# Mamba output projection: the residual goes through TensorE as an identity product, ScalarE copies the sum out, and TensorE waits for the gate's own signal

## Chip, cores and metric

One NeuronCore of a Trainium2 chip runs the whole program. The time is the device time of one execution in microseconds; the median of three runs of the kernel before is 5767.12 us (5765.01 to 5771.17). All data are float32.

## What is computed

The reference is four stacked blocks on x (4 sequences, 512 positions, width 256) with a context of 64 positions. The first block is a Mamba stack of four layers, and the change lies in it; the other three are transformer layers and stay as they are. The Mamba part, cut to what matters:

```python
p = silu(prepend_cond @ pre_w1) @ pre_w2
h = concatenate([p, x], axis=1)                 # 64 + 512 = 576 positions
for l in range(4):
    h = h + mamba_block(rmsnorm(h, norm_w[l]), ...)

def mamba_block(x, ...):
    xi, z = split(x @ ip_w.T)                   # 512 channels each
    xi = silu(causal_conv(xi) + cb)
    dt, Bm, Cm = split(xi @ xp_w.T)
    dt = softplus(dt @ dtp_w.T + dtp_b)
    # 16 states for every channel:
    #   state = exp(dt * A) * state + dt * Bm * xi ;  y += Cm * state
    y = y + xi * Dp
    y = y * silu(z)                             # the gate
    return y @ op_w.T                           # the output projection, then "h +" above
```

## The kernel before

Channels (or the model's 256 features, in KD = 2 halves) lie on the 128 partitions and the T = 576 positions along the free dimension. `hT` (named "stream" in the profile) holds h, the residual stream, in SBUF for all four sequences. The work is cut into 16 units (4 layers x 4 sequences), and the unit n is scanned in window n. A window has NJ = 32 steps, numbered j: 2 halves h of 256 channels (HC = 1152 elements per partition) times 16 states. In every step

- VectorE makes the drive (`drive`, L620, writes U in PSUM) and then runs the recurrence (`recur`, L628, writes the step's UH buffer in SBUF),
- ScalarE has made the decay factors DA for it (`decay`, L507; the decay for step j + 2 is issued in step j and may run four scans ahead),
- GpSimd multiplies UH by Cm (L561) while VectorE is in a later step,
- TensorE adds the result to Y in PSUM by a product with the identity IDENT (`add_up`, L357). `add_up(j - 2)` is issued in step j.

There are five UH buffers (four from step 20 on), so scan j waits until the sum of the step that last used its buffer is done; there are four DA buffers. Into the same window n every engine's queue has the preparation of unit n + 1 (`prep_step`, `prep_read`: norm, input projection, convolution, softplus) and the end of unit n - 1 woven in by hand: `PREP_AT` and `END_AT` say at which j. Each queue is a fixed program order and all ordering between engines goes by counting semaphores.

The end of a unit is the gate and the output projection. The gate (`gate`, L635) multiplies half the Y sums by silu(z) into ZS; half 0 is gated at j = 17 of the unit's own window, half 1 at j = 2 of the next one. The first `add_up` of the following half overwrites Y, so it waits for the gate. The output projection (`project`, two uses "O", m = 0 at j = 6 and m = 1 at j = 8 of the next window) writes PAIR, one pair of PSUM banks that all preparation products share too: every use waits on `s_free`, which the reader of the use before raises. Its product rows all show L313, the line of the helper `halves`. On VectorE `add(m)` (L642) adds PAIR to the residual at j = 7 and j = 9 and raises `s_free`, and after m = 1 `s_tail`, which the next read of that part of the stream waits for. Window 0 scans and has no end part; windows 1 to 15 have both; window 16 is only the end of unit 15. After it come the final RMS norm and the transformer layers.

Of the kernel before, what the change touches and what calls it, by code (L numbers as in the profile page):

```python
# [10 lines left out]
P = 128  # L11
# [90 lines left out]
def mamba_stack(nc, hT, IDENT, wa, wb, x_t, ctx_t, pre_w, ones, fin_norm):  # L102
# [3 lines left out]
    with ctx:  # L106
# [8 lines left out]
        def step(name):  # L115
            steps.append(sem(name))
            return steps[-1]
# [59 lines left out]
        s_scan = step("s_scan")  # L177
        s_hc = step("s_hc")
        s_y = step("s_y")
        s_gate = step("s_gate")  # L180
        s_add = step("s_add")
        s_yv = step("s_yv")
        s_tail = step("s_tail")
# [6 lines left out]
        def half(ap):  # L190
            return ap.rearrange("p (a n) -> p a n", a=2)
# [16 lines left out]
        with nc.Block() as block:  # L208
# [65 lines left out]
            def _(pe):  # L274
# [23 lines left out]
                def body(n, scan, prep, end):  # L298
                    uses, base = window_uses(prep, end), before(n, N_PREP, N_END)
                    par = n % 2  # L300
                    nxt = n + 1
                    npar = nxt % 2
                    done = [0]

                    def use(kind, i):
                        assert uses[done[0]] == (kind, i)
                        if scan or end or done[0]:
                            pe.wait_ge(s_free, START + base + done[0])
                        done[0] += 1

                    def halves(out_rows, lhs, rhs, start, stop):
                        for a in range(2):
                            mm = pe.matmul(PAIR[0:out_rows, a, 0:HT], lhs, rhs(a), start=start, stop=stop)  # L313
                        return mm

                    def cut(ap):
                        return lambda a: ap[:, a * HT:(a + 1) * HT]

                    def prep_step(kind, i):
                        use(kind, i)  # L320
                        if kind == "ms":
                            pe.wait_ge(s_sq, START + nxt + 1)
                            for k in range(KD):
                                mm = halves(P, ONES[:, :], cut(HN[:, k, :]), k == 0, k == KD - 1)
                        if kind == "xz":
                            if i == 0:
                                pe.wait_ge(s_wa, 16 * nxt + 16)
                                pe.wait_ge(s_hn, START + nxt + 1)
                            for k in range(KD):
                                mm = halves(P, w_in[:, k, i * P:(i + 1) * P], cut(HN[:, k, :]), k == 0, k == KD - 1)  # L330
                        if kind == "cv":
                            pe.wait_ge(s_xi, START + nxt * KI + i + 1)
                            if i == 0:
                                pe.wait_ge(s_pad, START + nxt + 1)
                                pe.wait_ge(s_dg, START + nxt // NB + 1)
                            for j in range(DC):
                                mm = halves(P, DG[:, i, j, :],
                                            lambda a, j=j: XPAD[:, i, j + a * HT:j + (a + 1) * HT], j == 0, j == DC - 1)
                        if kind == "xp":
                            pe.wait_ge(s_xs, START + nxt + 1)  # L340
                            for k in range(KI):
                                mm = halves(NXP, w_xp[:, k, :],
                                            lambda a, k=k: XS[:, bass.ds(npar * (KI * T) + k * T + a * HT, HT)],
                                            k == 0, k == KI - 1)
                        if kind == "dt":
                            if i == 0:
                                pe.wait_ge(s_bcf, START + nxt + 1)
                            mm = halves(P, w_dto[:, i * P:(i + 1) * P], cut(BCF[NBC:NXP, :]), True, True)
                        mm.then_inc(s_full, 1)

                    def add_up(j, of):
                        h, s = j // DS, j % DS
                        if s == 0:
                            pe.wait_ge(s_gate, START + 2 * of + h)
                        pe.wait_ge(s_hc, START + of * NJ + j + 1)
                        for a, b in YSEG:
                            mm = pe.matmul(Y[:, a:b], IDENT[:, :], UH[:, SLOT[j], a:b],  # L357
                                           start=(s == 0), stop=(s == DS - 1), skip_group_check=True)
                        mm.then_inc(s_y, 1)
                        if s == 0:  # L360
                            x = of % 2 * (KI * T) + h * HC
                            for c, a, b in DSEG:
                                pe.matmul(Y[:, a:b], DD[:, of // NB % 2, h * HK + c, :], XS[:, x + a:x + b],
                                          start=False, stop=False, skip_group_check=True)

                    def project(m):
                        use("O", m)
                        if m == 0:
                            pe.wait_ge(s_yv, START + 2 * n)
                            pe.wait_ge(s_wb, 16 * n)  # L370
                        epar = (n - 1) % 2
                        for k in range(KI):
                            mm = halves(P, w_out[:, k, m * P:(m + 1) * P],
                                        lambda a, k=k: ZS[:, bass.ds(epar * (KI * T) + k * T + a * HT, HT)],
                                        k == 0, k == KI - 1)
                        mm.then_inc(s_full, 1)

                    for j in range(NJ):
                        if end and j < 2:
                            add_up(NJ - 2 + j, n - 1)  # L380
                        for kind, i in slot_uses(j, prep, end):
                            if kind == "O":
                                project(i)
                            else:
                                prep_step(kind, i)
                        if scan and j >= 2:
                            add_up(j - 2, n)
# [11 lines left out]
            def _(act):  # L399
# [12 lines left out]
                def body(n, scan, prep, end):  # L412
# [26 lines left out]
                    def prep_read(kind, i):  # L439
# [24 lines left out]
                        if kind == "dt":  # L464
# [9 lines left out]
                            if i == KI - 1:  # L474
                                own(act.activation(ALOG[:, :], WA[:, A_LOG:A_COLS], ACT.Exp))
                                act.activation(NEGA[:, bass.ds(npar * (KI * DS), KI * DS)], ALOG[:, :], ACT.Copy,
                                               scale=-1.0).then_inc(s_nega, 1)

                    def diagonals(h):
                        if h == 0:  # L480
                            act.wait_ge(s_wa, 16 * nxt + 16)
                        for c in range(h * HK, h * HK + HK):
                            for j in range(DC):
                                w = A_CONV + c * DC + j
                                act.activation(DG[:, c, j, :], IDENT[:, :], ACT.Copy, scale=WA[:, w:w + 1])
                            ins = act.activation(DD[:, nxt // NB % 2, c, :], IDENT[:, :], ACT.Copy,
                                                 scale=DV[:, nxt // NB, c:c + 1])
                        if h:
                            ins.then_inc(s_dg, 1)
# [27 lines left out]
                    for j in range(NJ):  # L517
# [8 lines left out]
                        if prep and j in (2, 3) and nxt % NB == 0:  # L526
                            diagonals(j - 2)
                        for kind, i in slot_uses(j, prep, end):
                            if kind != "O":
                                prep_read(kind, i)  # L530
                    assert not prep or step[0] == k0, step
                act.wait_ge(s_zero, START + 3)
# [33 lines left out]
            def _(dve):  # L566
                def body(n, scan, prep, end):
# [63 lines left out]
                    def gate(of, h, at):  # L631
                        dve.wait_ge(s_y, START + of * NJ + DS * (h + 1))
                        dve.wait_ge(s_zs, START + of + 1)
                        z = ZS[:, bass.ds(at + h * HC, HC)]
                        dve.tensor_tensor(z, Y[:, 0:HC], z, ALU.mult).then_inc(s_yv, 1)  # L635
                        dve.wait_ge(s_yv, START + 2 * of + h + 1)
                        dve.sem_inc(s_gate, 1)

                    def add(m):
                        dve.wait_ge(s_full, START + base + uses.index(("O", m)) + 1)  # L640
                        h = hT[:, m, bass.ds(((n - 1) % NB) * T, T)]
                        dve.tensor_tensor(half(h), half(h), pair, ALU.add).then_inc(s_add, 1)  # L642
                        dve.wait_ge(s_add, START + (n - 1) * KD + m + 1)
                        dve.sem_inc(s_free, 1)  # L644
                        if m == KD - 1:
                            dve.sem_inc(s_tail, 1)

                    if scan:
                        dve.wait_ge(s_dt, START + n + 1)
                    for j in range(NJ):  # L650
# [7 lines left out]
                        if prep and j == 3:  # L658
                            norm()
                            pad()  # L660
                        if end and j in (7, 9):
                            add((j - 7) // 2)
                        if prep and j in SOFTPLUS:
                            softplus(*SOFTPLUS[j])
                    assert step[0] == (k_prep if prep else 0), step
# [990 lines left out]
```

## Time and profile before

| | us |
|---|---|
| median of 3 runs | 5767.12 |
| profiled execution | 5772.53 |
| its span on the core | 5770.7 |
| VectorE busy over the span | 3934.4 (68%) |
| TensorE busy over the span | 5049.1 (87%) |
| ScalarE busy over the span | 2275.0 (39%) |
| GpSimd busy over the span | 2549.6 (44%) |

The shares mix two stages: the Mamba stage ends at about 2520 us, the transformer layers fill the rest. The chain of work that ended last, as the profile gives it, adds up to 56% of the span and so covers only the transformer part; for the Mamba stage the timeline and the groups of instructions have to be read instead. In the forty slices of the page VectorE's digit is 9 from the second slice to the seventeenth.

### The profile page before, as it was taken

Reading aid. Unit: us, or ns where it says so; the run is one execution under the profiler, and the core shown is the slowest. Engines: PE = TensorE matmul, PEld = TensorE weight load, DVE = VectorE, ACT = ScalarE, POOL = GpSimd, SP = SyncE. Lnnn points to the kernel's source line nnn. Section 1 sums busy time; section 2 is a strip of 40 time slices with the busy share of each in tenths; the row PEclk is TensorE's granted clock in tenths of the full one; section 3 lists DMA queues with packets and bytes.
Section 4 is the critical chain, followed back from the end, with each engine's and each line's share of the span. In section 5 each row is a group of like instructions: output and inputs, shape, how many; then the busy total and the mean of one; then the engine's idle time right before and its main releaser. Section 6 shows DMA issues by size and latency. Waiting matters only on the chain.

```text
span 5770.7 us, 53704 instructions
## 1 busy us (share of the span) xinstructions
PE 5049.1 (87%) x18992; PEld 2658.1 (46%) x18992; DVE 3934.4 (68%) x3924; ACT 2275.0 (39%) x3972; POOL 2549.6 (44%) x1292
## 2 busy tenths in 40 slices
PE   6888888888888888669998799999978999999889
PEld 3445555455555555334444444444444444444444
DVE  2999999999999999946665515555454155554541
ACT  4555545555555554324343223333322133333221
POOL 1555555555555555527773004666400056664000
PEclk8999999999999999879999899999999999999999
DMA  2334433444344344310001000000101000001000
GB/s 82 139 141 142 145 135 136 144 144 143 141 142 146 141 145 140 133 46 1 1 1 37 26 11 1 1 1 1 44 1 37 0 1 1 1 1 44 1 0 15
DMA packets 94440, 376.70 MB, mean 65 GB/s; under 512 B 13025, under 2 KB 14433, under 8 KB 91233
## 3 DMA queue, kind: packets, MB, share of 16 engines
q1 hardware_dynamic: 94176, 373.26, 18.3%
q8 instruction: 157, 2.57, 0.2%
q14 instruction: 107, 0.87, 0.0%
HBM read 369.94 MB, written 3.28 MB: 65 GB/s over the span
## 4 chain that ended last, share of the span: by engine, by line
PE 45%; DVE 6%; POOL 2%; ACT 2%; issue 1%; DMA 0%; SPq 0%; ACTq 0%; DVEq 0%
PE PS L1010 6%; PE PS L1020 6%; PE PS L1034 6%; PE PS L989 5%; PE PS L1176 5%; PE PS L1185 3%; PE PS L1142 3%; PE PS L998 3%; PE PS L1044 2%; POOL PA L957 2%; PE PS L1116 2%; PE PS L1125 1%; DVE CST L1476 1%; DVE PA L1478 1%; PE PS L968 1%; DVE PA L1489 1%
## 5 line engine op out<-in xcount | busy, mean ns | idle before, releaser
L561 POOL TENSOR_TENSOR UH<-UH,BC 128x1152 f32<-128x1152 f32 x512 | 1343.0, 2623 | 1124.4 <-DVE U L620 1124.4
L957 POOL TENSOR_SCALAR PA<-PA,INV 128x512 f32<-128x512 f32 x768 | 1188.5, 1563 | 1296.5 <-DVE INV L1408 1296.5
L357 PE MATMUL Y<-UH,ident_sb 128*128 128x512 f32 (+1 forms) x3072 | 1180.1, 528 | 262.9 <-POOL UH L561 211.4
L628 DVE TENSOR_TENSOR_SCAN UH<-DA,U 128x1152 f32<-128x1152 f32 x512 | 1307.2, 2553 | 21.2 <-ACT DA L507 3.8
L357 PEld LDWEIGHTS Y<-UH,ident_sb 128*128 128x128 f32 x3072 | 593.0, 203 | 891.2 <-issue 571.2
L507 ACT ACTIVATE DA<-DT,NEGA 128x575 f32<-128x575 f32 x1024 | 722.9, 764 | 484.8 <-DVEq L612 259.9
L1247 ACT ACTIVATE PA<-PS,NMX 128x512 f32<-128x512 f32 x768 | 520.4, 682 | 981.4 <-DVE NMX L1402 968.5
L620 DVE TENSOR_TENSOR U<-DTX,BC 128x1152 f32<-128x1152 f32 x512 | 701.5, 1370 | 60.3 <-DVE stream L642 8.0
L1402 DVE TENSOR_REDUCE NMX<-PS 128x2 f32<-128x1024 f32 x384 | 468.0, 1219 | 296.4 <-PE PS L1010 296.4
L1417 DVE COPY VP<-PS 128x512 f32<-128x512 f32 x768 | 491.8, 681 | 15.0 <-PE PS L1020 14.6
L1020 PEld LDWEIGHTS PS<-ident_sb,PA 128*128 128x128 f32 x3072 | 329.4, 142 | 317.0 <-issue 214.7
L1020 PE MATMUL PS<-ident_sb,PA 128*128 128x128 f32 x3072 | 438.3, 282 | 9.4 <-POOL PA L957 8.6
L1010 PE MATMUL PS<-QK 64*128 64x512 f32 (+1 forms) x1536 | 435.4, 644 | 4.8 <-issue 2.5
L1034 PE MATMUL PS<-VP 128*64 128x256 f32 (+1 forms) x3072 | 373.9, 385 | 4.2 <-DVE VP L1417 2.5
L989 PE MATMUL PS<-HN,W 128*128 128x512 f32 x640 | 309.8, 606 | 54.9 <-ACTq L1240 52.0
L1394 DVE TENSOR_SCALAR QK<-PS,VEC 128x512 f32<-128x512 f32 x80 | 64.8, 810 | 347.1 <-PE PS L989 347.1
L313 PE MATMUL PAIR<-HN,WA 128*128 128x288 f32 x1024 | 280.4, 418 | 21.8 <-DVE HN L588 6.4
L1176 PE MATMUL PS<-HN,VP 128*128 128x512 f32 x640 | 288.6, 592 | 4.5 <-issue 4.5
L313 PE MATMUL PAIR<-XPAD,DG 128*128 128x288 f32 x1024 | 259.8, 406 | 3.3 <-ACTq L457 1.8
L1034 PEld LDWEIGHTS PS<-VP 128*64 128x64 f32 (+1 forms) x3072 | 202.2, 128 | 123.8 <-issue 38.1
L313 PEld LDWEIGHTS PAIR<-HN,WA 128*128 128x128 f32 x1024 | 189.6, 195 | 73.7 <-DVEq L644 8.0
L1519 DVE SCALAR_TENSOR_TENSOR QK<-PS,VEC,QK 128x512 f32<-128x512 f32 x64 | 48.1, 751 | 250.2 <-ACT QK L1326 250.2
(124 smaller groups left out, 5249.3 us busy)
## 6 DMA issues: line engine op xcount, KB each, us to landing
BC<-bc_rows SPq DMA_DIRECT2D x512, 576.0 KB, 3.7
WA<-mamba_a SPq DMA_DIRECT2D x16, 1421.0 KB, 7.4
W<-pair_w SPq DMA_DIRECT2D x6, 3072.0 KB, 10.6
WB<-mamba_b SPq DMA_DIRECT2D x16, 514.0 KB, 5.0
VP<-ff_w SPq DMA_DIRECT2D x2, 3072.0 KB
WO<-out_w SPq DMA_DIRECT2D x4, 1024.0 KB
stream<-x_t SPq DMA_DIRECT2D x2, 1024.0 KB, 6.7
VP<-ff_w SPq DMA_DIRECT2D x2, 1024.0 KB
```

Source lines behind the costliest of these rows:

```text
L313: mm = pe.matmul(PAIR[0:out_rows, a, 0:HT], lhs, rhs(a), start=start, stop=stop)
L357: mm = pe.matmul(Y[:, a:b], IDENT[:, :], UH[:, SLOT[j], a:b], start=(s == 0), stop=(s == DS - 1), skip_group_check=True)
L507: ins = act.activation(DA[:, j % NDA, c * T + 1:(c + 1) * T], DT[:, bass.ds(par * (KI * T) + cc * T + 1, T - 1)], ACT.Exp, scale=NEGA[:, b ...
L561: pool.tensor_tensor(h, h, BC[:, j % NBB, 1, :].unsqueeze(1).broadcast_to([P, HK, T]), ALU.mult).then_inc(s_hc, 1)
L620: dve.tensor_tensor(u, x, BC[:, j % NBB, 0, :].unsqueeze(1).broadcast_to([P, HK, T]), ALU.mult).then_inc(s_u, 1)
L628: dve.tensor_tensor_scan(UH[:, SLOT[j], :], DA[:, j % NDA, :], U[:, 0:HC], 0.0, ALU.mult, ALU.add).then_inc(s_scan, 1)
L957: pool.tensor_scalar(PR[:, n % 3, j, :], PR[:, n % 3, j, :], INV[:, n % 4, j:j + 1], None, ALU.mult).then_inc(s_ps, 1)
L989: mm = pe.matmul(PS[:, B_J, :], w_tile(l, "qk".index(kind), t, k), HN[:, k, b * S0:(b + 1) * S0], start=(k == 0), stop=(k == KD - 1))
L1010: mm = pe.matmul(PS[:, B_S + 2 * (n % 2) + j, :], Q[r:r + HW[l], tt % 2, qt * P:(qt + 1) * P], K[r:r + HW[l], tt % 2, :], start=True, stop ...
L1020: mm = pe.transpose(PS[:, B_T + j, kt * P:(kt + 1) * P], PR[:, n % 3, j, kt * P:(kt + 1) * P], IDENT[:, :])
L1034: mm = pe.matmul(PS[r:r + HW[l], B_V, half * 256:(half + 1) * 256], VT[:, tt // QT % 2, kt, c:c + HW[l]], PT[:, hh % 2, kt, j, :], start=( ...
L1176: mm = pe.matmul(PS[:, 2 * (f % 2) + g, :], w1[:, k, c:c + P], HN[:, k, b * S0:(b + 1) * S0], start=(k == 0), stop=(k == KD - 1))
```

## The change

The last product of each projection use no longer closes the sum. A product of IDENT with the residual itself follows into the same PAIR banks and closes it, so PAIR then holds h + y @ op_w. ScalarE copies PAIR over the residual (`stream(m)`), in its own queue at steps 6 and 8, and raises `s_free` and `s_tail`. VectorE's `add` is gone. VectorE's gate no longer waits for its own completion to raise a second semaphore `s_gate`; TensorE's first sum of a half waits on `s_yv`, which the gate instruction raises itself.

```diff
-                            pe.wait_ge(s_gate, START + 2 * of + h)
+                            pe.wait_ge(s_yv, START + 2 * of + h)
...
                         for k in range(KI):
                             mm = halves(P, w_out[:, k, m * P:(m + 1) * P],
                                         lambda a, k=k: ZS[...],
-                                        k == 0, k == KI - 1)
+                                        k == 0, False)
+                        mm = halves(P, IDENT[:, :], cut(hT[:, m, bass.ds(((n - 1) % NB) * T, T)]), False, True)
                         mm.then_inc(s_full, 1)
...
+                    def stream(m):
+                        full("O", m)
+                        act.activation(half(hT[:, m, bass.ds(((n - 1) % NB) * T, T)]), pair, ACT.Copy).then_inc(s_add, 1)
+                        act.wait_ge(s_add, START + (n - 1) * KD + m + 1)
+                        act.sem_inc(s_free, 1)
+                        if m == KD - 1:
+                            act.sem_inc(s_tail, 1)
...
-                            if kind != "O":
+                            if kind == "O":
+                                stream(i)
+                            else:
                                 prep_read(kind, i)
...
                         dve.tensor_tensor(z, Y[:, 0:HC], z, ALU.mult).then_inc(s_yv, 1)
-                        dve.wait_ge(s_yv, START + 2 * of + h + 1)
-                        dve.sem_inc(s_gate, 1)
-
-                    def add(m):
-                        dve.wait_ge(s_full, START + base + uses.index(("O", m)) + 1)
-                        h = hT[:, m, bass.ds(((n - 1) % NB) * T, T)]
-                        dve.tensor_tensor(half(h), half(h), pair, ALU.add).then_inc(s_add, 1)
-                        dve.wait_ge(s_add, START + (n - 1) * KD + m + 1)
-                        dve.sem_inc(s_free, 1)
-                        if m == KD - 1:
-                            dve.sem_inc(s_tail, 1)
...
-                        if end and j in (7, 9):
-                            add((j - 7) // 2)
```

VectorE's queue in window 1 of the kernel before, from the drive of step 2 over the gate and the two adds (L635 is the gate, L642 the adds, L620 drives, L628 scans):

```order
96 L620 TENSOR_TENSOR U<-DTX,BC 128x1152 [waits s_scan,s_bc2]
97 L628 SCALAR_TENSOR_TENSOR UH<-DA,U 128x1152 [waits s_y,s_da,s_u]
98 L635 TENSOR_TENSOR ZS<-Y,ZS 128x1152 [waits s_zs,s_y]
99 L620 TENSOR_TENSOR U<-DTX,BC 128x1152 [waits s_yv,s_scan,s_bc3]
...
111 L628 SCALAR_TENSOR_TENSOR UH<-DA,U 128x1152 [waits s_y,s_da,s_u]
112 L642 TENSOR_TENSOR stream<-stream,PAIR 128x576 [waits s_full]
113 L620 TENSOR_TENSOR U<-DTX,BC 128x1152 [waits s_add,s_scan,s_bc0]
...
116 L628 SCALAR_TENSOR_TENSOR UH<-DA,U 128x1152 [waits s_y,s_da,s_u]
117 L642 TENSOR_TENSOR stream<-stream,PAIR 128x576 [waits s_full]
118 L620 TENSOR_TENSOR U<-DTX,BC 128x1152 [waits s_add,s_scan,s_bc2]
```

The same stretch of VectorE's queue in the changed kernel, whose lines are ten higher here:

```order
96 L630 TENSOR_TENSOR U<-DTX,BC 128x1152 [waits s_scan,s_bc2]
97 L638 SCALAR_TENSOR_TENSOR UH<-DA,U 128x1152 [waits s_y,s_da,s_u]
98 L645 TENSOR_TENSOR ZS<-Y,ZS 128x1152 [waits s_zs,s_y]
99 L630 TENSOR_TENSOR U<-DTX,BC 128x1152 [waits s_scan,s_bc3]
...
111 L638 SCALAR_TENSOR_TENSOR UH<-DA,U 128x1152 [waits s_y,s_da,s_u]
112 L630 TENSOR_TENSOR U<-DTX,BC 128x1152 [waits s_scan,s_bc0]
113 L638 SCALAR_TENSOR_TENSOR UH<-DA,U 128x1152 [waits s_y,s_da,s_u]
114 L630 TENSOR_TENSOR U<-DTX,BC 128x1152 [waits s_scan,s_bc1]
```

The adds and their waits are gone, and the drive behind the gate no longer waits on s_yv. TensorE's queue in the same window, kernel before, from the last preparation product ahead of the projection to the first one behind it:

```order
200 L313 MATMUL PAIR<-HN,WA 128x288 [waits s_free]
201 L313 MATMUL PAIR<-HN,WA 128x288 x3
...
205 L313 MATMUL PAIR<-ZS,WB 128x288 [waits s_wb,s_yv,s_free]
206 L313 MATMUL PAIR<-ZS,WB 128x288 x7
207 L357 MATMUL Y<-UH,ident_sb 128x512 [waits s_hc]
...
213 L313 MATMUL PAIR<-ZS,WB 128x288 [waits s_free]
214 L313 MATMUL PAIR<-ZS,WB 128x288 x7
...
221 L313 MATMUL PAIR<-HN,WA 128x288 [waits s_free]
```

And in the changed kernel:

```order
200 L312 MATMUL PAIR<-HN,WA 128x288 [waits s_free]
201 L312 MATMUL PAIR<-HN,WA 128x288 x3
...
205 L312 MATMUL PAIR<-ZS,WB 128x288 [waits s_wb,s_yv,s_free]
206 L312 MATMUL PAIR<-ZS,WB 128x288 x7
207 L312 MATMUL PAIR<-stream,ident_sb 128x288 x2
208 L356 MATMUL Y<-UH,ident_sb 128x512 [waits s_hc]
...
214 L312 MATMUL PAIR<-ZS,WB 128x288 [waits s_free]
215 L312 MATMUL PAIR<-ZS,WB 128x288 x7
216 L312 MATMUL PAIR<-stream,ident_sb 128x288 x2
...
223 L312 MATMUL PAIR<-HN,WA 128x288 [waits s_free]
```

Each projection has grown by two products; nothing else moved on TensorE.

## Rows read from the trace of the kernel before

**Rows 1.** Windows view: length, busy time of each engine, PEclk, DMA share, GB/s.

```profile
100.00:2400.00 2300.00, 1945.17 (x6222) 1143.05 (x6221) 2216.26 (x1253) 1190.65 (x1607) 1293.42 (x493) 0.92 0.40 140
```

**Rows 2.** Groups on VectorE from 100 to 2400 us: busy us, mean ns, idle before.

```profile
L620 DVE TENSOR_TENSOR U<-DTX,BC 128x1152 f32<-128x1152 f32 x495 | 678.3, 1370 | 58.4 <-DVE stream L642 8.0 <-DVE ZS L635 6.4 <-DVEq L612 3.9
...
L635 DVE TENSOR_TENSOR ZS<-Y,ZS 128x1152 f32<-128x1152 f32 x30 | 39.9, 1331 | 0.0
...
L642 DVE TENSOR_TENSOR stream<-stream,PAIR 128x576 f32<-128x576 f32 x30 | 21.8, 728 | 0.0
```

**Rows 3.** Timeline of VectorE around both adds, window 6: start, length, instruction.

```profile
1034.87 1.37 DVE L620 TENSOR_TENSOR U<-DTX,BC 128x1152 f32<-128x1152 f32 x1
...
1038.74 0.73 DVE L642 TENSOR_TENSOR stream<-stream,PAIR 128x576 f32<-128x576 f32 x1
1039.68 1.37 DVE L620 TENSOR_TENSOR U<-DTX,BC 128x1152 f32<-128x1152 f32 x1 [0.21 <-DVE stream L642]
...
1043.74 1.37 DVE L620 TENSOR_TENSOR U<-DTX,BC 128x1152 f32<-128x1152 f32 x1
...
1047.61 0.73 DVE L642 TENSOR_TENSOR stream<-stream,PAIR 128x576 f32<-128x576 f32 x1
1048.66 1.37 DVE L620 TENSOR_TENSOR U<-DTX,BC 128x1152 f32<-128x1152 f32 x1 [0.32 <-DVE stream L642]
```

**Rows 4.** Timeline of VectorE: norm, gate and softplus, each with the drive behind it.

```profile
1021.16 1.61 DVE L588 SCALAR_TENSOR_TENSOR HN<-stream,WA,RSTD 128x576 f32<-128x576 f32 x2
1022.71 1.34 DVE L620 TENSOR_TENSOR U<-DTX,BC 128x1152 f32<-128x1152 f32 x1
...
1080.94 1.33 DVE L635 TENSOR_TENSOR ZS<-Y,ZS 128x1152 f32<-128x1152 f32 x1
1082.49 1.37 DVE L620 TENSOR_TENSOR U<-DTX,BC 128x1152 f32<-128x1152 f32 x1 [0.21 <-DVE ZS L635]
...
1142.44 1.36 DVE L605 SCALAR_TENSOR_TENSOR XPAD<-XPAD 128x1152 f32<-128x1152 f32 x1
1143.84 1.37 DVE L620 TENSOR_TENSOR U<-DTX,BC 128x1152 f32<-128x1152 f32 x1
```

**Rows 5.** Timeline of TensorE around both projections, window 6.

```profile
1030.99 4.05 PE L313 MATMUL PAIR<-ZS,WB 128*128 128x288 f32 x16
1034.87 4.04 PE L357 MATMUL Y<-UH,ident_sb 128*128 128x512 f32 x12
1039.58 4.15 PE L313 MATMUL PAIR<-ZS,WB 128*128 128x288 f32 x16 [0.67 <-DVEq L644]
1043.56 4.04 PE L357 MATMUL Y<-UH,ident_sb 128*128 128x512 f32 x12
1048.45 1.72 PE L313 MATMUL PAIR<-HN,WA 128*128 128x288 f32 x6 [0.85 <-DVEq L644]
```

**Rows 6.** Timeline of ScalarE, window 6: decay of step 11, and a copy of PAIR.

```profile
1038.85 1.44 ACT L507 ACTIVATE DA<-DT,NEGA 128x575 f32<-128x575 f32 x2 [2.62 <-DVE UH L628]
...
1050.70 0.65 ACT L446 ACTIVATE XPAD<-PAIR 128x576 f32<-128x576 f32 x1 [5.59 <-PE PAIR L313]
```

**Rows 7.** Timeline of VectorE, window 6: the scans of steps 23 and 24.

```profile
1104.18 2.55 DVE L628 TENSOR_TENSOR_SCAN UH<-DA,U 128x1152 f32<-128x1152 f32 x1
...
1108.24 2.55 DVE L628 TENSOR_TENSOR_SCAN UH<-DA,U 128x1152 f32<-128x1152 f32 x1
```

**Rows 8.** Timeline of ScalarE: the decays of steps 23 and 24.

```profile
1098.73 2.77 ACT L507 ACTIVATE DA<-DT,NEGA 128x575 f32<-128x575 f32 x4
```

**Rows 9.** Timeline of TensorE: the sum of step 20.

```profile
1101.54 2.21 PE L357 MATMUL Y<-UH,ident_sb 128*128 128x512 f32 x6
```

**Rows 10.** Timeline of the last window, all engines: first projection, its add, the second projection.

```profile
2480.16 4.12 PE L313 MATMUL PAIR<-ZS,WB 128*128 128x288 f32 x16 [1.50 <-issue]
2484.31 0.75 DVE L642 TENSOR_TENSOR stream<-stream,PAIR 128x576 f32<-128x576 f32 x1 [4.26 <-PE PAIR L313]
2485.18 4.15 PE L313 MATMUL PAIR<-ZS,WB 128*128 128x288 f32 x16 [0.90 <-DVEq L644]
```

More of the change, by code:

```diff
@@ L179, in mamba_stack @@
         s_y = step("s_y")
-        s_gate = step("s_gate")
         s_add = step("s_add")
```

## The prediction, made before the run

> **What bounds the kernel now.** I began with the busy time of each engine over the Mamba stage. From 100 to 2400 us VectorE is busy 2216.3 of 2300 us, that is 96%, while TensorE has 1945.2, GpSimd 1293.4 and ScalarE 1190.7 [rows 1]. The whole program's 68% for VectorE hides this, because the transformer layers dilute it. Next I asked what VectorE's idle time there is made of. The groups show it in crumbs: the drive, L620, has 58.4 us before 495 instructions, of which 8.0 lie behind the adds, 6.4 behind the gates and 3.9 behind softplus; the rest is the regular gap between scan and drive [rows 2]. No other engine is named as a large releaser. So in this stage the VectorE queue itself is the clock. The timeline shows its beat: the drive of step 8 starts at 1039.68 and that of step 9 at 1043.74, 4.06 us later, and no other engine is in between [rows 3]. What leaves this queue comes off the time, as long as nobody else becomes late. The transformer layers start after the stage and keep their length.
>
> **The adds leave VectorE.** A step without an add takes 4.06 us from drive to drive. The step with the first add takes 1039.68 - 1034.87 = 4.81, the one with the second 1048.66 - 1043.74 = 4.92 [rows 3]. That is 0.75 and 0.86, or 1.61 us a window, although the instruction itself lasts 0.73: it starts before the scan's end is reported, but the drive behind it waits for the add's completion and for one or two separate semaphore increments (0.21 and 0.32 idle). Fifteen windows have both a scan and an end part, so 15 x 1.61 = **24.2 us** come off.
>
> **The gates lose their own wait.** The gate lasts 1.33, but the drive behind it starts 1.55 us after the gate starts, 0.21 or 0.22 after its end [rows 4]. Without the wait on itself and the increment, two neighbours bound what is left. Behind softplus the drive also waits for its predecessor's completion, but with no separate increment, and starts 1143.84 - 1142.44 = 1.40 after it, 0.04 after its end; that would save 0.18. Behind the norm there is no wait for completion at all, and the drive starts 1.55 after the norm's start, with 1.61 of work reported, so 0.06 before its end [rows 4]; that would save 0.28. The changed gate is of the second kind, since the drive's remaining waits (scan, BC rows) are met long before. I take 0.27. There are 16 gates of half 0 and 15 of half 1 with a drive behind them: 31 x 0.27 = **8.4 us**, between 5.6 and 8.7.
>
> Here a rule of the Trainium skill speaks against the gate's part. The rows above show 0.21 behind the gate against 0.04 behind softplus. The page "VectorE: DVE Perf Modes", section "The DRAIN you can't avoid", says that an instruction waits for the pipeline to empty anyway, and that "the semaphore costs nothing extra here". By that the gate's part would be worth nothing, and the sum would be 22.4 instead of 30.8. The trace bears it out for the plain wait (0.04) and not for the wait with an increment of its own (0.21), so I keep 8.4.
>
> **TensorE's new work.** A projection is 16 recorded products, and the next group starts 1034.87 - 1030.99 = 3.88 later, 0.243 each [rows 5]. The identity product of the residual adds two float32 products of 288 columns, four records: 0.97 us each time, 1.94 a window. What hides it is that TensorE waited in just these places for VectorE's add to free PAIR: 0.67 before the second projection and 0.85 before the preparation product behind it, 1.52 together [rows 5]. Placed in order: projection 0 from 1030.99 to 1035.84, the two sums to 1039.71, projection 1 (before: 1039.58) to 1044.56, the two sums to 1048.43, next product (before: 1048.45). TensorE comes out of the stretch where it did. VectorE, however, is then 1.61 + 0.27 = 1.9 us ahead, so TensorE's lead over the scans shrinks by up to that.
>
> How much lead is there? The nearest case in the window is scan 24, which needs the UH buffer whose last sum, step 20, ends at 1101.54 + 2.21 = 1103.75; the scan starts at 1108.24 [rows 7, 9]. The lead is 4.5 us. If the whole 1.9 and the second gate's 0.27 came off it, 2.3 would be left. I cost the added products at nothing; without that cover each microsecond would cost 15 over the stage. PAIR also comes free earlier than before, since ScalarE copies it at once and not behind a scan.
>
> **ScalarE's new work.** Two copies of PAIR to SBUF of 128x576, like the one at L446 that takes 0.65 [rows 6]: 1.3 us a window on an engine busy 1190.7 of 2300 [rows 1]. What matters is what stands behind a copy that waits. In the queue, `stream(0)` stands ahead of the decay for step 9 and `stream(1)` ahead of the decay for step 11. The latter ran at 1038.85 [rows 6]; now it waits for projection 1 (1044.6 plus its tail), the copy ends near 1045.6 and the decay near 1047.1. Scan 11 starts, on the beat of rows 3, at 1048.66 + 4.06 + 1.40 = 1054.1 before, so near 1052.2 now: 5.1 us of lead instead of 13.8. The tightest decay is that of step 23: two decays share the 2.77 from 1098.73, so the first ends near 1100.1, and scan 23 starts at 1104.18 [rows 7, 8]. Its lead of 4.0 shrinks by the same 2.2 at most, to 1.8. It is behind TensorE's convolutions and ScalarE's SiLU, and it still holds. Cost: nothing.
>
> **TensorE's first sums of a half** hear the gate one increment earlier, some 0.1 us. TensorE isn't the bound, so nothing.
>
> **The last window** has no scan to hide anything. Projection, reader, projection, reader stand in line [rows 10]. Each projection grows by 0.97, each copy replaces an add of 0.75 by 0.65: 2 x (0.97 - 0.1) = **1.8 us** slower.
>
> **Sum.** -24.2 - 8.4 + 1.8 = -30.8. The profiled execution took 5772.53 with a span of 5770.7, so 1.8 lies outside the span. Its successor should have a span near 5739.9 and take 5741.7. The median of the runs shown, 5767.12, lies 5.4 below the profiled one, which I take over: 5767.1 - 30.8 = **5736.3 us**. Runs of before differ by 6 us among each other; a difference under 0.2%, 11.5 us, could hardly be told from none.
>
> **Rivals.**
>
> 1. *The wait behind the gate stays.* The gap after the gate is then the pipeline's own. Against it stands 0.04 behind softplus [rows 4]. Time: 5767.1 - 22.4 = 5744.7. Chance 0.10.
>
> 2. *ScalarE's copies slow VectorE.* They read PSUM and write SBUF while scans and drives run, where VectorE itself did it before. The rows show drives at a mean of 1.370 with ScalarE busy half of the time [rows 1, 2], so contention is small. If each of 30 copies cost a VectorE instruction 0.23, 7 us would go back: 5743. Chance 0.05.
>
> 3. *The lead is used up, the time hardly moves.* The scans come to wait for sums or for decays around steps 20 to 24. To fall inside 0.2%, (30.8 - 11.5) / 15 = 1.3 us must be lost in each window; with 1.8 left there, the lead must have shrunk by 3 us more than I work out, for instance because the SiLU and the decays queue up behind later TensorE work. Time from 5755.6 to 5767. Chance 0.05.
>
> 4. *Slower: the decays behind a waiting copy.* Place: ScalarE's queue in step 8, where the decay for step 11 now stands behind projection 1. It decides once that projection ends more than 5.1 us later than 1044.6. That would come about if TensorE ran this stretch at the lower of its clock levels, 1.2 GHz: 2 x 4.85 for each projection and 2 x 3.87 for the sums between puts its end at 1058.1, the decay's at 1060.5 against a scan at 1052.2, so 8.3 are lost and 2.1 won in each of 15 windows: +93, plus 1.8 in the tail, less what the gate of half 0 gives: near 5860. Against it stands that products there run at 0.243 each [rows 5], and that TensorE now waits less in this stretch, not more. Mean granted clock is 0.92 [rows 1]. Chance 0.03.
>
> **How the numbers follow.** The forecast has 0.77. It and the first two rivals are all faster by more than 0.2%: 0.92. Rival 3 gives the same: 0.05, rival 4 slower: 0.03. The gate's bounds alone move the sum from 28.0 to 31.1. Around the forecast I add the runs' own spread of some 4 us to both sides, and a little more below for beats that the rows round: 5727. Above, the range reaches over rivals 1 and 2 with part of that spread: 5748.
>
> **What would show it.** In the profile after, VectorE's adds are absent and drive to drive is 4.06 in steps 7 and 9 (adds right). The drive starts within 0.05 us of the gate's end or before it (gate right); 0.2 behind it speaks for rival 1. The projection is a group of 20 records, 4.85 to the next group, and no TensorE idle time has VectorE's increment as its releaser (cover right). Scans show no idle time released by ScalarE or TensorE (lead right; otherwise rivals 3 or 4). A window, from the drive of step 0 to the next such drive, shrinks by 2.1 us. I would be wrong if that period shrank less while VectorE's busy time fell as expected; then a wait at L638 would name the engine. Or the transformer part, untouched, could shift by a few us with TensorE's clock.

## The result and the profile after

The changed kernel takes 5743.82 us (median of 5 runs, 5739.52 to 5745.58), against 5767.17 us (5 runs, 5765.01 to 5771.17). The ratio is 0.9958 with a 95% interval of 0.9943 to 0.9972, which is 16 to 33 us; the medians give 23 us, the ratio 24. The forecast was 30.8 us faster, 5736.3, with a range of 5727 to 5748. The profiled execution took 5742.71 with a span of 5740.9, 29.8 below the profiled one of before. Not all of that belongs to the change. From the first drive of window 0 to the memset of the tile KB, with which the transformer layers begin, the kernel before needs 2522.67 - 112.25 = 2410.4 us and the changed one 2496.11 - 109.43 = 2386.7, so 23.7 less. The other 6 lie ahead of the stage (first drive at 109.4 instead of 112.3) and in the transformer layers (3244.8 instead of 3248.1), which no edit touches. In the twelve profiles of this study these layers take 3241.9 to 3249.2 us.

The groups on VectorE from 100 to 2400 us in the changed kernel, columns as in [rows 2]:

```profile
L630 DVE TENSOR_TENSOR U<-DTX,BC 128x1152 f32<-128x1152 f32 x502 | 687.4, 1369 | 48.4 <-DVEq L622 4.2 <-DVE UH L638 1.9
...
L645 DVE TENSOR_TENSOR ZS<-Y,ZS 128x1152 f32<-128x1152 f32 x31 | 41.5, 1338 | 4.6 <-PE Y L356 4.6
```

The adds are gone, and so is the idle time behind adds and gates. But ahead of the gate, L645, where VectorE had no idle time before [rows 2], it now has 4.6 us that ended with a sum of TensorE (L356). That is a new wait. The timeline of VectorE in window 6, gate of half 1 and then the drives of steps 7 and 8, answers to [rows 3, 4]:

```profile
1003.50 1.33 DVE L645 TENSOR_TENSOR ZS<-Y,ZS 128x1152 f32<-128x1152 f32 x1
1004.75 1.35 DVE L630 TENSOR_TENSOR U<-DTX,BC 128x1152 f32<-128x1152 f32 x1
...
1022.30 1.37 DVE L630 TENSOR_TENSOR U<-DTX,BC 128x1152 f32<-128x1152 f32 x1
...
1026.36 1.37 DVE L630 TENSOR_TENSOR U<-DTX,BC 128x1152 f32<-128x1152 f32 x1
```

The step with the first add takes 4.06 now (it took 4.81), and the drive starts 1.25 after the gate's start instead of 1.55, 0.08 before the gate's end. TensorE in the same window, answering to [rows 5]:

```profile
1020.37 4.05 PE L312 MATMUL PAIR<-ZS,WB 128*128 128x288 f32 x16
1024.26 1.13 PE L312 MATMUL PAIR<-stream,ident_sb 128*128 128x288 f32 x4
1025.23 4.04 PE L356 MATMUL Y<-UH,ident_sb 128*128 128x512 f32 x12
1029.10 4.05 PE L312 MATMUL PAIR<-ZS,WB 128*128 128x288 f32 x16
1032.99 1.13 PE L312 MATMUL PAIR<-stream,ident_sb 128*128 128x288 f32 x4
1033.96 4.04 PE L356 MATMUL Y<-UH,ident_sb 128*128 128x512 f32 x12
1037.83 2.11 PE L312 MATMUL PAIR<-HN,WA 128*128 128x288 f32 x8
```

From the first projection to the preparation product behind the second pass 1037.83 - 1020.37 = 17.46 us, exactly as in window 6 of the kernel before (1048.45 - 1030.99). The added 0.97 a time is visible (1025.23 - 1024.26), and the two waits for VectorE are gone; no row has idle time. Window 6 of the kernel before is not like all others, though. In its window 5 the same stretch reads:

```profile
884.39 4.05 PE L313 MATMUL PAIR<-ZS,WB 128*128 128x288 f32 x16
...
892.15 4.05 PE L313 MATMUL PAIR<-ZS,WB 128*128 128x288 f32 x16
...
900.24 1.97 PE L313 MATMUL PAIR<-HN,WA 128*128 128x288 f32 x7 [0.17 <-DVEq L644]
```

TensorE is 1.6 us later behind the gate there (first projection 16.8 after it, 15.2 in window 6), so it hardly waits for the adds, and the stretch takes 15.85. Of the fourteen windows 1 to 14 of the kernel before only 2, 4, 6, 8 and 10 have the waits of 1.52; the other nine have 0 to 0.32 and stretches of 15.5 to 16.0. In the changed kernel the stretch takes 17.46 in all fourteen, 1.5 to 1.9 more than in those nine.

ScalarE in window 6 of the changed kernel:

```profile
1025.43 0.65 ACT L481 ACTIVATE stream<-PAIR 128x576 f32<-128x576 f32 x1 [4.58 <-PE PAIR L312]
1026.20 2.77 ACT L515 ACTIVATE DA<-DT,NEGA 128x575 f32<-128x575 f32 x4
1034.16 0.65 ACT L481 ACTIVATE stream<-PAIR 128x576 f32<-128x576 f32 x1 [5.19 <-PE PAIR L312]
1035.00 2.77 ACT L515 ACTIVATE DA<-DT,NEGA 128x575 f32<-128x575 f32 x4 [0.19 <-ACT stream L481]
```

ScalarE does wait 4.6 and 5.2 us for the projections, and decays stand behind it in pairs, but no scan of windows 1 to 15 shows idle time put down to them. Now step 17 of this window, the place of the new wait, all engines:

```profile
1062.88 1.37 DVE L630 TENSOR_TENSOR U<-DTX,BC 128x1152 f32<-128x1152 f32 x1
...
1063.07 4.04 PE L356 MATMUL Y<-UH,ident_sb 128*128 128x512 f32 x12
...
1064.29 2.55 DVE L638 TENSOR_TENSOR_SCAN UH<-DA,U 128x1152 f32<-128x1152 f32 x1
...
1067.15 1.36 DVE L645 TENSOR_TENSOR ZS<-Y,ZS 128x1152 f32<-128x1152 f32 x1 [0.31 <-PE Y L356]
1068.42 1.36 DVE L630 TENSOR_TENSOR U<-DTX,BC 128x1152 f32<-128x1152 f32 x1
```

The sums of steps 14 and 15 run as one group without a gap and end at 1067.11; the gate starts 0.04 later. It should have started 0.08 before the scan's end (1066.84), at 1066.76, so VectorE loses 0.39. In the kernel before the sum of step 15 of this window reads:

```profile
1077.19 2.21 PE L357 MATMUL Y<-UH,ident_sb 128*128 128x512 f32 x6 [1.30 <-POOL UH L561]
```

It ended at 1079.40, 1.54 us ahead of the gate (1080.94 [rows 4]), after TensorE had waited 1.30 for GpSimd. The lead is 1.5 in all fourteen windows there.

How much is lost differs between windows, and the difference begins far earlier. TensorE where its sums resume after the gate of half 1, first in window 6, then in window 8:

```profile
1004.89 2.96 PE L356 MATMUL Y<-UH,ident_sb 128*128 128x512 f32 x6 [3.45 <-DVE ZS L645]
1007.64 3.20 PE L362 MATMUL Y<-XS,DD 128*128 128x512 f32 x8
```

```profile
1297.50 2.21 PE L356 MATMUL Y<-UH,ident_sb 128*128 128x512 f32 x6 [2.99 <-DVE ZS L645]
1299.54 2.22 PE L362 MATMUL Y<-XS,DD 128*128 128x512 f32 x8
```

The windows view of these stretches (columns as in [rows 1]):

```profile
1004.80:1010.60 5.80, 5.71 (x14) 2.99 (x15) 5.76 (x7) 1.60 (x3) 2.61 (x1) 0.71 0.39 127
1297.40:1301.50 4.10, 4.00 (x14) 2.19 (x15) 4.07 (x4) 1.61 (x3) 2.62 (x1) 1.00 0.42 143
1010.00:1068.00 58.00, 58.00 (x211) 37.24 (x210) 55.86 (x31) 25.65 (x37) 36.81 (x14) 1.00 0.42 152
```

In window 6 TensorE resumes at a mean granted clock of 0.71, so partly at 1.2 GHz, after waits of 5.80 us ahead of the norm's product and 3.45 for the gate; in window 8 it resumes at 1.00, 2.4 GHz, after waits of 3.80 and 2.99. That costs 5.8 against 4.1 us, and from there to 1068 it is busy 58.00 of 58.00 us: nothing absorbs the late start. The fourteen windows sort without exception. Where the first input product comes 7.4 us after the gate of half 1 starts (7, 8, 10, 11, 13, 14), the sum is done 1.35 ahead of the gate of half 0 and VectorE loses nothing. Where it comes 9.1 after (1 to 6) it loses 0.37 to 0.40, and where it comes 10.3 or 10.4 after (9 and 12) 1.58 and 1.32. Together 5.2 us. The mean granted clock from the first sum behind the gate to that input product is 1.00 in the first group, 0.78 in the second and 0.66 to 0.67 in the third.

The last window, answering to [rows 10]:

```profile
2450.33 4.12 PE L312 MATMUL PAIR<-ZS,WB 128*128 128x288 f32 x16 [1.50 <-issue]
2454.28 1.13 PE L312 MATMUL PAIR<-stream,ident_sb 128*128 128x288 f32 x4
2455.45 0.65 ACT L481 ACTIVATE stream<-PAIR 128x576 f32<-128x576 f32 x1 [27.44 <-PE PAIR L312]
2456.20 4.15 PE L312 MATMUL PAIR<-ZS,WB 128*128 128x288 f32 x16 [0.79 <-ACTq L483]
```

One projection follows the other after 5.87 us, it was 5.02 [rows 10].

### The profile page after: what moved, and what is told of

It reads as the page before. It is cut to its first block, busy times and chain, and to the rows that moved or that the text cites. A ratio compares the mean times of both kernels' runs of the same rounds, so it can differ in the third digit from the quotient of the medians.

```text
span 5740.9 us, 53927 instructions
## 1 busy us (share of the span) xinstructions
PE 5059.7 (88%) x19120; PEld 2676.5 (47%) x19120; DVE 3911.5 (68%) x3892; ACT 2293.0 (40%) x4004; POOL 2553.2 (44%) x1292
## 4 chain that ended last, share of the span: by engine, by line
PE 45%; DVE 6%; POOL 2%; ACT 2%; issue 1%; DMA 0%; SPq 0%; ACTq 0%; DVEq 0%
PE PS L1007 6%; PE PS L1017 6%; PE PS L1031 6%; PE PS L986 5%; PE PS L1173 5%; PE PS L1182 3%; PE PS L1139 3%; PE PS L995 3%; PE PS L1041 2%; POOL PA L954 2%; PE PS L1113 2%; PE PS L1122 1%; DVE CST L1473 1%; DVE PA L1475 1%; PE PS L965 1%; DVE PA L1486 1%
## 5 line engine op out<-in xcount | busy, mean ns | idle before, releaser
L356 PE MATMUL Y<-UH,ident_sb 128*128 128x512 f32 (+1 forms) x3072 | 1174.3, 527 | 226.9 <-POOL UH L571 172.2
L356 PEld LDWEIGHTS Y<-UH,ident_sb 128*128 128x128 f32 x3072 | 592.4, 203 | 847.5 <-issue 571.9
L630 DVE TENSOR_TENSOR U<-DTX,BC 128x1152 f32<-128x1152 f32 x512 | 701.1, 1369 | 49.5 <-DVEq L622 4.2
## 6 DMA issues: line engine op xcount, KB each, us to landing
W<-pair_w SPq DMA_DIRECT2D x6, 3072.0 KB, 10.5
```

Source lines behind the costliest of these rows:

```text
L630: dve.tensor_tensor(u, x, BC[:, j % NBB, 0, :].unsqueeze(1).broadcast_to([P, HK, T]), ALU.mult).then_inc(s_u, 1)
```

## Experiments

All times are medians; each ratio is to the kernel before on the same chip. To keep the scatter of the transformer layers out, the text also gives the length of the fourteen windows from the first drive of window 1 to the first drive of window 15 in the profile: 2077.2 us before (2339.1 - 261.9) and 2052.1 after (2310.9 - 258.8).

**Each part alone.** First the gate's part on the kernel before:

```diff
-                            pe.wait_ge(s_gate, START + 2 * of + h)
+                            pe.wait_ge(s_yv, START + 2 * of + h)
...
                         dve.tensor_tensor(z, Y[:, 0:HC], z, ALU.mult).then_inc(s_yv, 1)
-                        dve.wait_ge(s_yv, START + 2 * of + h + 1)
-                        dve.sem_inc(s_gate, 1)
```

> The kernel before with the gate's part alone: no wait of VectorE on its own gate, no separate increment, TensorE waits on the gate's own signal; the adds stay on VectorE. Theory: each of 31 drives behind a gate starts 0.297 us earlier, as in the profile after (1.249 us from the gate's start against 1.546), and no gate has to wait for a sum, so 9.2 us come off: about 5758, a ratio of 0.9984. Rival (the gap is the pipeline's own, or its gain is lost elsewhere): 5767, ratio 1.000.

Measured: 5763.93 against 5769.31, ratio 0.9990 (0.9982 to 0.9999). The windows take 2069.5, 7.8 less (28 of the gates lie in them, 28 x 0.297 = 8.3). All drives behind a gate start 1.248 after it, and the gate of half 0 waits for no sum. The mechanism holds; of its 9.2 the medians show 5.4 and the ratio 5.8, and the interval, 0.6 to 10.4 us, has 9.2 in it. In this profile the last gate also came 1.1 us later behind the last drive (10.06 for 8.99), because the sums ahead of it ran in part at the lower clock.

Then the residual's part, with the gate's lines as before:

```diff
+                        dve.wait_ge(s_yv, START + 2 * of + h + 1)
+                        dve.sem_inc(s_gate, 1)
```

> The changed kernel with the gate's wait and the separate increment put back: only the residual has moved. Theory: 24.2 us come off for the adds, 1.8 come back in the last window, and the gates of half 0 wait for the sum of step 15 less often than in the changed kernel, since VectorE is 0.3 us less ahead: 0.1 us in some windows where it was 0.4, together 2 to 3 us instead of 5. Time 5747 to 5748, ratio 0.9965. Rival (the residual's part is eaten up by the longer projection): within 5 us of before, 5762 or more.

Measured: 5750.05, ratio 0.9965 (0.9953 to 0.9977); windows 2056.4, 20.8 less. It was 2 us slower than expected. The gate of half 0 lost 1.50 in window 1 and 0.11 to 0.14 in windows 3, 13 and 14, and nothing elsewhere: 1.9 in all. Parts apart give 5.4 + 19.3 = 24.7 in the medians, together 23 to 24.

**Is the new wait TensorE's backlog?** In the changed kernel one preparation product moves behind the sum of step 15:

```diff
-           16: ("xz", 4), 18: ("cv", 2), 20: ("cv", 3), ...
+           18: ("cv", 2), 19: ("xz", 4), 20: ("cv", 3), ...
```

> The changed kernel with one preparation product, input projection 4 of the next unit, taken from step 16 to step 19, so that TensorE reaches the sum of step 15 by 1.94 us earlier. Theory: the gates of half 0, which wait 0.4 to 1.6 us for that sum in eight windows of the profile after, wait no more; 4.9 us come off the changed kernel: 5739, ratio to before 0.9951. Rival (those waits are not TensorE's backlog, or they come back at a later scan): 5744, ratio 0.9959.

Measured: 5736.47, ratio 0.9940 (0.9928 to 0.9953); windows 2046.4, 5.7 less than in the changed kernel. Around step 17 of window 6 its timeline reads:

```profile
1063.68 2.21 PE L356 MATMUL Y<-UH,ident_sb 128*128 128x512 f32 x6 [1.48 <-POOL UH L571]
...
1067.43 1.33 DVE L645 TENSOR_TENSOR ZS<-Y,ZS 128x1152 f32<-128x1152 f32 x1
```

TensorE again waits for GpSimd before the sum in this window, as it did before the change, and the gate has no idle time in any window but the last, the end of unit 15. The fourteen windows now take what the two parts alone should leave: 2077.2 - 14 x 1.61 - 28 x 0.297 = 2046.4. The margin isn't wide: in windows 2 and 7, where TensorE resumed latest (first input product 10.5 after the gate), the sum ends only 0.23 and 0.26 ahead of the next gate.

The same edit on the kernel before is the control:

> The kernel before with input projection 4 of the next unit moved from step 16 to step 19, nothing else. Theory: in the kernel before the gate of half 0 does not wait for the sum of step 15 but in the last scan window (0.37 us), so the move brings 0.4 us at most: 5769, ratio 1.000. Rival (the move is good for a reason of its own, as the 7 us between the changed kernel with and without it, 2 more than its waits, could suggest): several us faster, 5762.

Measured: 5769.06 against 5769.99, ratio 0.9999 (0.9990 to 1.0009), windows 2077.2 as before. The move is worth something only after the change.

Both kernels, changed and changed with the move, then ran side by side:

> The changed kernel once more, on one chip with the next one. Theory: ratio to before 0.9958, near 5745; rival: the same.

> The changed kernel with input projection 4 in step 19 once more, now beside the changed kernel. Theory: its waits at the gate of half 0 are gone, 5 us, and the first scan window is some 2 us longer, as in its first profile: 3 to 7 us under the changed kernel, ratio to before 0.9945 to 0.9952. Rival (the first difference was scatter between jobs): within 2 us of the changed kernel.

Measured: 5744.76, ratio 0.9959 (0.9945 to 0.9972), and 5735.59, ratio 0.9945 (0.9933 to 0.9958). The windows take 2053.2 and 2046.6. The medians differ by 9.2, more than the 6.6 of the windows; the ratios' intervals still overlap by themselves, but both comparisons and both pairs of profiles point the same way. This is the fastest version here that computes the whole reference: about 33 us, 0.55 to 0.6%, under the kernel before.

**More and less work on TensorE.** The identity product twice:

```diff
+                        mm = halves(P, IDENT[:, :], cut(hT[:, m, bass.ds(((n - 1) % NB) * T, T)]), False, False)
                         mm = halves(P, IDENT[:, :], cut(hT[:, m, bass.ds(((n - 1) % NB) * T, T)]), False, True)
```

> The changed kernel with the identity product of the residual issued twice, so that the residual is added twice in the output; it doubles TensorE's added work. Theory (the gate of half 0 waits for the sum of step 15 because TensorE has no slack from step 3 to there): the wait at step 17 grows by the added 1.94 us in the nine windows that have little lead in the profile after, and to some 0.6 in the six that have a lead of 1.35, together 21 us; the last window takes 1.9 more. Time near 5767. Rival (the products are hidden): about 2 us more than the changed kernel, 5746.

Measured: 5754.72, ratio 0.9973 (0.9963 to 0.9984), windows 2063.8. The windows are 11.7 us longer than the changed kernel's 2052.1 for another 1.94 of TensorE's work in each (by the medians, each against before on its own chip, 15.3 us faster instead of 23.4): the rival's 2 us are wrong, and my 23 too. In its window 6:

```profile
1065.76 4.04 PE L356 MATMUL Y<-UH,ident_sb 128*128 128x512 f32 x12
...
1069.84 1.36 DVE L646 TENSOR_TENSOR ZS<-Y,ZS 128x1152 f32<-128x1152 f32 x1 [0.55 <-PE Y L356]
```

Every window now loses at this gate, but by two sizes: 0.63 in nine of them and 1.8 to 2.3 in windows 1 and 9 to 12. Nine windows resumed at the full clock here, not six (and the profile after has eight windows with little lead, not the nine of my expectation). The two sizes are those I had expected (0.6 and 2.33); how many windows fall on either side is not a property of the edit, since the repeat of the unchanged code (the run of the changed kernel above) had four that resumed at full clock (8, 9, 12, 13) where its first profile had six.

Without the identity product:

```diff
-                        mm = halves(P, IDENT[:, :], cut(hT[:, m, bass.ds(((n - 1) % NB) * T, T)]), False, True)
```

> The changed kernel without the identity product: the residual is left out of the sum and ScalarE copies the projection alone. It gives the price of TensorE's share. Theory: the waits of the gate of half 0 vanish (4.9 us) and the last window loses 1.9: near 5737. Rival (TensorE's added work costs only the last window): 5742.

Measured: 5733.01, ratio 0.9937 (0.9921 to 0.9953), windows 2046.6, no gate but the last one waits. In this profile TensorE resumed at the lower clock in ten of the fourteen windows (mean granted clock 0.78 to 0.80 up to the first input product, which comes 8.9 to 9.1 after the gate), and the sum of step 15 still ended 1.5 ahead of every gate. So without the product the lower clock makes no gate wait, and in the six windows of the changed kernel that resume at full clock the single product doesn't either: the waits of the changed kernel take both. TensorE's share costs the changed kernel 5.5 in the windows and 1.9 in the last one (from gate to norm 12.5 us against 14.4). With the product at its place and the preparation moved, the windows take the same 2046.4 to 2046.6: moved like that, the identity product is free but for the tail.

**Does it matter who copies?** The identity product on TensorE, but VectorE copies at its old places:

```diff
-                        dve.tensor_tensor(half(h), half(h), pair, ALU.add).then_inc(s_add, 1)
+                        dve.tensor_copy(half(h), pair).then_inc(s_add, 1)
```

> The kernel before (gate and increment as there) with the residual added by the identity product on TensorE, but VectorE copies PAIR out at its old places, steps 7 and 9. Theory (the gain is the time that leaves VectorE's queue, not the cheaper operation): a copy takes what the add took, 0.73 us, TensorE's longer projections fill its old waits and the rest is hidden; only the last window grows by 1.9. Time 5771, ratio 1.0003. Rival (a copy is much cheaper than an add on VectorE): several us faster than before.

Measured: 5772.21 against 5769.99, ratio 1.0004 (0.9994 to 1.0013), windows 2077.2. The groups on VectorE show why:

```profile
L643 DVE COPY stream<-PAIR 128x576 f32<-128x576 f32 x30 | 21.9, 731 | 0.0
```

A copy takes 731 ns where the add took 728 [rows 2]. Making the operation simpler buys nothing; leaving the queue does.

**The gate's wait without its increment:**

```diff
                         dve.tensor_tensor(z, Y[:, 0:HC], z, ALU.mult).then_inc(s_yv, 1)
+                        dve.wait_ge(s_yv, START + 2 * of + h + 1)
```

> The changed kernel with VectorE's wait on its own gate put back, but no separate increment. Theory: the drive then starts as it does behind softplus, 0.04 us after the gate's end, 1.37 to 1.40 us after its start instead of 1.25: 31 x 0.13 = 4 us slower than the changed kernel, less what gates of half 0 wait less; near 5747. Rival by the rule that a semaphore costs nothing extra: the gap stays 1.25 and the time 5744.

Measured: 5746.24, ratio 0.9958 (0.9946 to 0.9971). The time can't tell it from the changed kernel, the profile can:

```profile
1070.11 1.36 DVE L645 TENSOR_TENSOR ZS<-Y,ZS 128x1152 f32<-128x1152 f32 x1 [0.18 <-PE Y L356]
1071.50 1.37 DVE L630 TENSOR_TENSOR U<-DTX,BC 128x1152 f32<-128x1152 f32 x1
```

The median distance from gate to drive is 1.366, between 1.249 and 1.546. So the wait for completion costs 0.12 and the separate increment 0.18. That makes 31 x 0.117 = 3.6 us, but where VectorE is slower by that, the gate of half 0 waits less (0.26 for 0.39 in most windows, 3.0 in all for 5.2), so part of it comes back: the windows take 2053.4, 1.3 more than in the changed kernel.

## Why the prediction came out as it did

- **The bound.** Right: VectorE's queue sets the Mamba stage, and what left it came off the time. The vector-copy run shows the reverse: same queue, same 2077.2 us.
- **The adds, 24.2 us.** Right in size. The part alone took 20.8 off the fourteen windows, where 14 x 1.61 = 22.5 were to be expected and 1.9 went to new gate waits.
- **The gates, 8.4 us.** Slightly too small in the profile: 31 x 0.297 = 9.2. The neighbour without a wait, the norm, was the right one to read. The Trainium skill (page "VectorE: DVE Perf Modes", section "The DRAIN you can't avoid") says of a chain of copies that "the semaphore costs nothing extra here"; for this pair, gate and drive, that does not hold. Here an own wait costs 0.12 and a separate increment 0.18, and the measurement decides.
- **TensorE's cover.** This is the term that the prediction had wrong. The four records of 0.243 were right, and in window 6 the placement too (17.44 us worked out, 17.46 measured). Two things failed. The first is the question how much lead there is, which the prediction answers with scan 24. I followed the sums only to the scans that wait for their buffer and forgot a second reader of the same sums: the gate of half 0 needs the sum of step 15 itself. The second is that the cover of 1.52 was read in window 6 alone. Nine of the fourteen windows of the kernel before have no more than 0.32 of it, because TensorE comes to it later (mean granted clock 0.66 to 0.80 from the first sum behind the gate to the first input product, against 1.00 in the other five). In such windows the products are hardly covered.
  In numbers: the sum ended 1.54 ahead of the gate. From the stretch to the end of that sum TensorE took 30.95 us before, with the wait of 1.30 (1048.45 to 1079.40), and takes 29.28 without it (1037.83 to 1067.11), so it had 1.54 + 1.67 = 3.2 us to give. VectorE's gain takes 1.9, and 1.3 is left (1.35 seen). That is a window that resumes at full clock. In a window like window 5 of the kernel before the stretch also grows, from 15.85 to 17.46, by 1.61, and the sum comes 0.3 too late (0.39 seen in windows 1 to 6). "I cost the added products at nothing" should have read 5 us. The margins at step 23 and 24 that I did give, 1.8 and 2.3 left, came out as 2.2 and 2.7 and never mattered.
- **ScalarE.** Right: copies of 0.65, no scan waits. The decay of step 11 keeps 5.2 us of lead where TensorE resumes at full clock (I gave 5.1), 3.5 in window 6 and 2.2 in the latest.
- **The last window, 1.8.** From the gate's start to the norm's first product it takes 14.4 instead of 12.7, so 1.7. Another 2.6 came in the profile after from products that ran at the lower clock: 1.1 from the sums ahead of the last gate (10.06 behind the last drive instead of 8.99), 1.5 from the norm's products (32.8 from the first of them to the KB memset instead of 31.3). The repeat of the changed kernel shows the second again (33.3) and not the first (8.99). The kernel before with the gate's part alone shows the first, with no product added there, so I put it down to TensorE's clock and not to a step of the change.
- **The sum.** Inside the stage the profile gives -24.2 - 9.2 + 4.8 (5.2 of gate waits, less 0.4 that the kernel before had) + 1.7, which is -26.9. With 2.6 for the clock in the tail and some 0.6 for single steps that took 0.35 longer it comes to -23.7. The rivals' mechanisms did not appear: the gap behind the gate closed, no VectorE instruction got longer (drives 1369 ns after, 1370 before), no scan waited. A mechanism that none of the four rivals names, nearest to rival 3 but at the gate and milder, took 5 of the 7.5 us by which I was too low. The rest is clock and scatter. That the time lies in the range is in part luck: the upper end, 5748, was set by rivals 1 and 2, which did not occur, and happened to have room for a wait that I hadn't seen.

That the low clock decides between 0 and 1.6 us per window of the changed kernel is read from the rows of all windows, in its profile, in its repeat and in the run with two identity products; no run here changed the clock alone. Why a window resumes at one level or the other stays open.

## What to carry to other kernels

When work leaves the bounding queue, list every consumer that this queue's instructions wait for, the direct readers of a result as well as those that wait for a buffer, and subtract the gain from each lead; the smallest lead decides, and it belongs to the slowest of the windows and not to the one looked at. The same holds for idle time that is to hide new work: here the window looked at had 1.52 us of it and nine of fourteen had next to none, which the profile before could have told. If a lead is short, the cure is often the order: here one preparation product moved three steps later made the added products free. On a full queue an instruction that waits for its predecessor's completion and then raises a semaphore by itself costs as much as the gap it makes, so let the producing instruction raise the signal that others wait for.

## What the hardware showed that I had not expected

A copy from PSUM is no cheaper on VectorE than an add with PSUM: 731 against 728 ns for 128x576. The drive behind the gate starts 0.08 us before the gate's reported end when nothing makes it wait. And TensorE, busy 58.00 of 58.00 us, carries a delay of 1.7 us, from products that ran in part at the lower clock, undiminished to the next place where somebody waits, nearly 60 us later.
